# The first residual of a four-layer graph network in one VectorE operation from PSUM, and a new order of work on four engines

## The chip, the cores and the metric

One core of a Trainium2 chip runs the whole program. The metric is the device time of one execution in microseconds (us), median of several. Five parts of the core matter here: TensorE (PE, matrix products; PEld is its weight load), VectorE (DVE), ScalarE (ACT), GpSimd (POOL) and the DMA queue that SyncE (SP) issues. Each runs its own list of instructions strictly in order; a semaphore wait stops everything behind it on that engine.

## The reference, cut to what matters

There are 32 graphs of 256 nodes with 256 features. Each passes four layers, and each layer ends in a residual and a normalization over the features (LN):

```
L0(x)  = (adj @ (x @ W0 + b0)) / rowsum(adj)
L1(x)  = relu((adj @ x) @ W1) * mask(x)
L2(x)  = relu(D^-1/2 (adj + I) D^-1/2 @ x @ W2 + b2),   D = rowsum(adj + I)
L3(x)  = relu(sum over k of  T^k x Wk + bk),  T = rownorm(adj * exp(leaky_relu(attention)))
x = LN(x + L0(x));  x = LN(x + L1(x));  x = LN(x + L2(x));  x = LN(x + L3(x))
```

The change is in the first line of the last group: x + L0(x), before LN. Because every row of adj divided by its row sum adds up to one, b0 can be added to x itself: the kernel computes y0 = (x + b0) + (adj @ (x W0)) / rowsum(adj).

## The kernel before, in words

**Tiles.** A graph is one tile of 128 partitions by 512 columns: two nodes per partition, 256 features each. Eight groups of four graphs ("slots" g = 0 to 3) are worked on. Each fp32 operand of a product is split into a high part (`_hi`, rounded to the fast fp32 format, copied by ScalarE) and a low part (`_lo`, the difference, made by VectorE or GpSimd), and `product` (lines 253 to 263) does lo*hi + hi*lo + hi*hi: 12 matmuls for one 256x256 product.

**Products.** `s1` = x W0, `s2` = adj (x W0) with a column of ones that gives the row sums, `s3`, `s4` = layer 1, `s5`, `s6` = layer 2, `s7` = transposes of x3, `s8a`, `s8b` = x3 by the four weight blocks of layer 3, `s9` = transposes for the attention logits, `s10`, `s11` = the two hops. PSUM has four `ring` banks, one for each slot, and two `pair` tiles of two banks; `pair` is shared in turn by s1, s2, s8a, s8b and s10.

**Stages.** One pass of the loop, `iteration(k)`, does the layers 2 and 3 of group k, the layers 0 and 1 of group k + 1 up to its `s5`, and `s1` of group k + 2. Before it stands `first_iteration` (layers 0 and 1 of group 0), behind it `last_iteration` (layers 2 and 3 of group 7). What sets the order on each engine is a list of calls written out by hand in these functions, one list for each engine; there is no planner in the kernel.

**The first residual.** `sums0` (VectorE, lines 984 to 987) takes the row sums from PSUM and makes the reciprocal `rinv`. `z0` (ScalarE, line 496) multiplies each of the two nodes by its reciprocal on the way from `pair` to X1. `x_bias` (GpSimd, line 751) has added b0 to x in X0, and for group 0 `first_x_bias` (VectorE, line 1065) does. `y0` (GpSimd, line 760) adds X1 to X0. `statistics(0, ...)` (line 975), `variance_eps` (980, 981), `power` (GpSimd, 767) and `norm0` (GpSimd, 782) normalize it to X1, from which `x1_hi` (ScalarE) and `x1_lo` (VectorE, 1008) feed `s3`. `z0_ready` also tells TensorE that a `pair` bank is free: `s2(2)` and `s2(3)` wait for z0 of slots 0 and 1, `s8a(0)` and `s8b(0)` for z0 of slots 2 and 3.

**Names in the rows.** Layers, groups and slots share names: `nod_lo` at line 1013 is `xd_lo` (feeds `s5`), `fea_lo` at 967 is `from_ring` on VectorE, `P<-pair,rinv,P` at 1047 is `q`, `X<-ring,X` at 1060 is `y3`, `adj_lo` at 755 is `adj_lo_part`, `adj_lo` at 806 is `diag_lo`, `mask` at 999 is `mask_of_x1`, `tmp` at 1034 is `leaky`, `W_lo` at 1083 is `weights_lo`, `X<-X,nmr,rstd` at 566 is `norm`.

**SP's queue** in a pass: four loads of xT for group k + 2 (each waits for `s1` of its slot), four of x (each waits for `x1_sum`), four of adj for layer 3, four of adj for group k + 2, and four stores of the output.

Of the kernel before, what the change touches and what calls it, by code (L numbers as in the profile page):

```python
# [25 lines left out]
P = 128  # L26
# [8 lines left out]
def build(nc, x, xT, adjT, w0, w1, w2, wk, wvT, aw, bv, ab, b0, b2, bk, out):  # L35
# [7 lines left out]
    with ExitStack() as ctx:  # L43
# [90 lines left out]
        xT_hi_ready, xT_ready = sem("xT_hi_ready"), sem("xT_ready")  # L134
# [118 lines left out]
        def _(pe):  # L253
# [23 lines left out]
            def s1(g, kn, first=False):  # L277
                pe.wait_ge(xT_ready, count(g, kn))
                if not first:
                    pe.wait_ge(Q_ready, count(2 + g // 2, kn - 2))  # L280
                elif kn == 1:
                    pe.wait_ge(z0_ready, count(2 + g // 2, 0))
# [94 lines left out]
            def first_iteration():  # L377
                for g in (0, 1):
                    s2(g, 0)
                attention_vectors()  # L380
                for g in (2, 3):
                    s2(g, 0)
                for g in (0, 1):
                    s1(g, 1, first=True)
                for g in (0, 1):
                    s3(g, 0, first=True)
                for g in (0, 1):
                    s4(g, 0)
                for g in (2, 3):
                    s3(g, 0, first=True)  # L390
                for g in (2, 3):
                    s4(g, 0)
                for g in (2, 3):
                    s1(g, 1, first=True)
                for g in range(SLOTS):
                    s5(g, 0, first=True)

            def iteration(k, ahead=True):
                for g in (0, 1, 2):
                    s6(g, k)  # L400
# [47 lines left out]
            def last_iteration(k):  # L448
                for g in range(SLOTS):
                    s6(g, k)  # L450
                s7(0, k)
                s8a(0, k, last=True)
                s7(1, k)
                s8b(0, k, last=True)
                s9(0, k)
                s8a(1, k, last=True)
                s7(2, k)
                s8b(1, k, last=True)
                s8a(2, k, last=True)
                s7(3, k)  # L460
                s9(1, k)
# [907 lines left out]
```

## Time and profile before

| | us |
|---|---|
| median of 3 runs (599.04 to 599.85) | 599.43 |
| the profiled execution | 597.33 |
| its span, first to last instruction | 595.5 |
| first `s6(0)` of a group starts, us from the start of the span | 61.09 |
| last one | 541.82 |
| busy: PE, DVE, POOL, ACT | 543.3, 536.2, 471.0, 425.3 |

The span is cut best where TensorE starts `s6(0)`, since that is the start of a pass: 61.09, 130.18, 199.24, 268.35, 337.77, 406.86, 476.84 and 541.82. The first piece is the start with group 0, then come six passes with `s1` ahead, one without, and the last group. Busy time of an instruction is from its start to its end; neighbours on VectorE and ScalarE overlap by about 0.08 us, so a group's busy time is a little more than the time that it takes from the engine. A matmul row of 0.28 us starts 0.12 us after the one ahead of it.

### The profile page before, as it was taken

Reading aid. Unit: us, or ns where it says so; the run is one execution under the profiler, and the core shown is the slowest. Engines: PE = TensorE matmul, PEld = TensorE weight load, DVE = VectorE, ACT = ScalarE, POOL = GpSimd, SP = SyncE. Lnnn points to the kernel's source line nnn. Section 1 sums busy time; section 2 is a strip of 40 time slices with the busy share of each in tenths; the row PEclk is TensorE's granted clock in tenths of the full one; section 3 lists DMA queues with packets and bytes.
Section 4 is the critical chain, followed back from the end, with each engine's and each line's share of the span. In section 5 each row is a group of like instructions: output and inputs, shape, how many; then the busy total and the mean of one; then the engine's idle time right before and its main releaser. Section 6 shows DMA issues by size and latency. Waiting matters only on the chain.

```text
span 595.5 us, 12249 instructions
## 1 busy us (share of the span) xinstructions
PE 543.3 (91%) x4044; PEld 512.1 (86%) x4044; DVE 536.2 (90%) x1213; ACT 425.3 (71%) x937; POOL 471.0 (79%) x575
## 2 busy tenths in 40 slices
PE   5687999999999999999999999998999999987983
PEld 5577998999899998999889998898889998887873
DVE  3779899999999999998999999998999989999666
ACT  5467788488866878578884878667785778756653
POOL 3799699888997799878997889887998788773243
PEclk9979999999999999999999999999999999999998
DMA  8613101431132300322014311324003210101001
GB/s 285 236 56 113 47 19 22 157 101 58 35 106 70 141 18 18 113 98 106 18 36 141 122 35 35 106 70 141 18 18 111 100 37 1 54 19 71 1 1 70
DMA packets 25222, 44.73 MB, mean 75 GB/s; under 512 B 3184, under 2 KB 3824, under 8 KB 25200
## 3 DMA queue, kind: packets, MB, share of 16 engines
q1 hardware_dynamic: 24336, 43.79, 22.1%
q10 hardware_dynamic: 864, 0.66, 0.3%
q8 instruction: 12, 0.20, 0.1%
q14 instruction: 10, 0.08, 0.0%
HBM read 36.05 MB, written 8.39 MB: 75 GB/s over the span
## 4 chain that ended last, share of the span: by engine, by line
PE 36%; DVE 29%; POOL 14%; issue 8%; ACT 8%; DMA 2%; SPq 2%; ACTq 0%; POOLq 0%; DVEq 0%
PE pair L260 8%; PE pair L262 8%; PE pair L261 8%; DVE nod_lo L1013 6%; POOL rstd L767 4%; PE ring L260 4%; ACT X L566 3%; DVE P L1047 3%; PE ring L262 3%; PE ring L261 3%; POOL tmp L789 3%; DVE ring L1055 3%; DVE stats L975 3%; DVE powin L980 2%; DMA xT_in<-xT_dram 2%
## 5 line engine op out<-in xcount | busy, mean ns | idle before, releaser
L767 POOL TENSOR_TENSOR rstd<-powin,minus_half 128x2 f32<-128x2 f32 (+1 forms) x128 | 107.9, 843 | 58.9 <-DVE nmean L981 58.9
L566 ACT ACTIVATE X<-X,nmr,rstd 128x256 f32<-128x256 f32 x192 | 103.5, 592 | 30.4 <-POOL nmr L776 30.1
L975 DVE BATCH_NORM_STATS2 stats<-X 128x6 f32<-128x512 f32 x128 | 89.5, 704 | 1.6 <-POOL X L760 1.2
L260 PE MATMUL ring<-adj_hi,nod_lo 128*128 128x256 f32 x256 | 74.9, 292 | 13.3 <-DVE X L1060 8.1
L260 PE MATMUL ring<-W_hi,fea_lo 128*128 128x256 f32 x256 | 72.5, 283 | 0.9 <-DVE fea_lo L967 0.8
L261 PE MATMUL ring<-adj_lo,nod_hi 128*128 128x256 f32 x256 | 73.0, 285 | 0.0
L262 PE MATMUL ring<-adj_hi,nod_hi 128*128 128x256 f32 x256 | 72.8, 284 | 0.0
L262 PE MATMUL ring<-W_hi,fea_hi 128*128 128x256 f32 x256 | 71.7, 280 | 0.0
L261 PE MATMUL ring<-W_lo,fea_hi 128*128 128x256 f32 x256 | 71.4, 279 | 0.0
L487 ACT ACTIVATE fea_hi<-ring 128x512 fp32r<-128x512 f32 x96 | 55.3, 591 | 22.2 <-PE ring L322 12.2
L967 DVE TENSOR_TENSOR fea_lo<-ring,fea_hi 128x512 fp32r<-128x512 f32 x96 | 63.8, 681 | 2.9 <-ACT fea_hi L487 2.6
L260 PEld LDWEIGHTS ring<-adj_hi,nod_lo 128*128 128x128 f32 x256 | 49.4, 193 | 16.1 <-DVE nod_lo L1013 12.5
L487 ACT ACTIVATE h_hi<-P 128x512 fp32r<-128x512 f32 x32 | 20.2, 633 | 55.1 <-DVE P L1047 55.1
L789 POOL TENSOR_TENSOR tmp<-tmp,adj_in 128x512 f32<-128x512 f32 x32 | 47.3, 1486 | 14.6 <-ACT tmp L551 14.6
L1013 DVE SCALAR_TENSOR_TENSOR nod_lo<-X,rstd,nod_hi 128x256 fp32r<-128x256 f32 x64 | 53.8, 882 | 1.3 <-ACT nod_hi L528 1.0
L260 PE MATMUL pair<-WB_hi,fea_lo 128*128 128x512 f32 x128 | 53.5, 418 | 0.2 <-DVE h_lo L995 0.2
L755 POOL TENSOR_TENSOR adj_lo<-adj_in,adj_hi 128x512 fp32r<-128x512 f32 x32 | 40.8, 1298 | 14.6 <-ACT adj_hi L487 14.6
L261 PE MATMUL pair<-WB_lo,fea_hi 128*128 128x512 f32 x128 | 50.6, 395 | 0.0
L760 POOL TENSOR_TENSOR X<-X 128x512 f32<-128x512 f32 x32 | 45.2, 1412 | 6.6 <-ACT X L496 5.9
L262 PE MATMUL pair<-WB_hi,fea_hi 128*128 128x512 f32 x128 | 50.4, 394 | 0.0
L260 PEld LDWEIGHTS ring<-W_hi,fea_lo 128*128 128x128 f32 x256 | 48.2, 188 | 1.7 <-issue 1.3
L261 PEld LDWEIGHTS ring<-adj_lo,nod_hi 128*128 128x128 f32 x256 | 49.6, 194 | 0.0
(109 smaller groups left out, 2125.8 us busy)
## 6 DMA issues: line engine op xcount, KB each, us to landing
adj_in<-adjT_dram SPq DMA_DIRECT2D x64, 256.0 KB, 3.2
xT_in<-xT_dram SPq DMA_DIRECT2D x32, 256.0 KB, 3.5
X<-x_dram SPq DMA_DIRECT2D x32, 256.0 KB, 2.6
out_dram<-X SPq DMA_DIRECT2D x32, 256.0 KB, 2.0
P<-wk_dram SPq DMA_DIRECT2D x3, 256.0 KB, 8.4
P<-w_dram SPq DMA_DIRECT2D x2, 256.0 KB, 8.0
X<-bk_dram SPq DMA_DIRECT2D x3, 128.0 KB, 7.8
P<-w_dram ACTq DMA_DIRECT2D x1, 256.0 KB, 3.9
```

The source lines that it names most:

```text
L260: mm(o, lhs(1, t, i), rhs(0, t), start=t == 0, stop=False)
L261: mm(o, lhs(0, t, i), rhs(1, t), start=False, stop=False)
L262: last = mm(o, lhs(0, t, i), rhs(0, t), start=False, stop=t == 1)
L487: return nc.scalar.activation(dst, src, ACT.Copy)
L566: last = nc.scalar.activation(nodes(X[min(l + 1, 3)][g])[:, t, :], nodes(X[l][g])[:, t, :], ACT.Identity, scale=rstd[l][g][:, t:t + 1], bi ...
L755: tt(adj_lo[g][:, :], adj_in[g][:, :], adj_hi[g][:, :], ALU.subtract).then_inc(adj_ready, 1)
L760: tt(X0[g][:, :], X0[g][:, :], X1[g][:, :], ALU.add).then_inc(y_ready[0][g], 1)
L767: tt(rstd[l][g][:, 0:n], powin[l][g][:, 0:n], minus_half[:, 0:n], ALU.pow).then_inc(rstd_ready[l], 1)
L789: tt(tmp[g][:, :], tmp[g][:, :], adj3_in[g][:, :], ALU.mult).then_inc(al_ready, 1)
L967: tt(fea_lo[g][:, :], ring[g][:, :], fea_hi[g][:, :], ALU.subtract).then_inc(ready, 1)
L975: nc.vector.bn_stats(stats[l][g][:, :], by_turns(X[l][g])).then_inc(st_ready[l], 1)
L1013: last = stt(nod_lo[g][:, t * F:(t + 1) * F], nodes(X2[g])[:, t, :], rstd[0][g][:, 2 + t:3 + t], nod_hi[g][:, t * F:(t + 1) * F], ALU.mult ...
```

## The change: what it does

`z0` on ScalarE and `y0` on GpSimd go. VectorE has a new `y0` of two operations: pair * rinv + X0, written over X0. It waits for `rinv0_ready` (made by its own `sums0`) and for the bias addition; `y0_done` takes the place of `z0_ready` and of `y_ready[0]` everywhere. The bias additions of group 0 count in a semaphore of their own, as do the first four low parts of xT. All calls of the four engines stand in a new order.

```diff
 # VectorE
+            def y0(g, kn, first=False):
+                dve.wait_ge(rinv0_ready, count(g, kn))
+                if first:
+                    dve.wait_ge(first_xb_ready, g + 1)
+                else:
+                    dve.wait_ge(xb_ready, count(g, kn - 1))
+                for t in range(2):
+                    half = nodes(X0[g])[:, t, :]
+                    last = stt(half, pair[g % 2][:, t, 0:F], rinv[g][:, t:t + 1], half, ALU.mult, ALU.add)
+                last.then_inc(y0_done, 1)
 # ScalarE
-            def z0(g, kn):
-                act.wait_ge(rinv0_ready, count(g, kn))
-                for t in range(2):
-                    last = nc.scalar.activation(nodes(X1[g])[:, t, :], pair[g % 2][:, t, 0:F], ACT.Identity,
-                                                scale=rinv[g][:, t:t + 1])
-                last.then_inc(z0_ready, 1)
 # GpSimd
-            def y0(g, kn):
-                pool.wait_ge(xb_ready, count(g, kn))
-                pool.wait_ge(z0_ready, count(g, kn))
-                tt(X0[g][:, :], X0[g][:, :], X1[g][:, :], ALU.add).then_inc(y_ready[0][g], 1)
 # TensorE: s2(2), s2(3); s8a(0), s8b(0) and the first s1 ahead in the same way
                 if g >= 2:
-                    pe.wait_ge(z0_ready, count(g - 2, kn))
+                    pe.wait_ge(y0_done, count(g - 2, kn))
```

The new order, as the calls now follow each other (n = k + 1; a number or letter in brackets is the slot, `..` a row of slots; "ring" is `from_ring`, "var" `variance_eps`, "stat" `statistics`, "ms" `mean_scale`):

```
TensorE, a pass: s6(0) s6(1) s2(0,n) s6(2) s2(1,n) s2(2,n) s7(0) s6(3) s2(3,n) s7(1) s8a(0) s8b(0) s9(0)
  s8a(1) s7(2) s3(0,n) s8b(1) s8a(2) s4(0,n) s9(1) s9(2) s7(3) s8b(2) s8a(3) s3(1,n) s9(3) s3(2,n) s8b(3)
  s4(1,n) s4(2,n) s10(0) s10(1) s3(3,n) s10(2) s4(3,n) s10(3) s11(0) s11(1) s11(2) s1(0) s1(1) s11(3)
  s5(0,n) s5(1,n) s1(2) s5(2,n) s5(3,n) s1(3)
VectorE, start of a pass: h_lo(0..2) y2(0) y2b(0) h_lo(3) stat(2,0) y2(1) sums0(0) y2b(1) var(2,0) y0(0)
  y2(2) stat(2,1) stat(0,0) sums0(1) sums0(2) var(2,1) var(0,0) y0(1) y0(2) ring(x3T,0) y2b(2) sums0(3)
  y0(3) stat(2,2) var(2,2) stat(0,1) p0(0) ...
VectorE, end of a pass: ... q(3) var(1,3) z3(0) y3(0) z3(1) stat(3,0) z3(2) y3(1) y3(2) stat(3,1) xd_lo(0)
  var(3,0) var(3,1) xd_lo(1) stat(3,2) z3(3) var(3,2) xd_lo(2) y3(3) stat(3,3) var(3,3) xd_lo(3) ring(t2,0..3)
ScalarE, start: h_hi(0) h_hi(1) h_hi(2) adj_hi(0) xT_hi(0) h_hi(3) adj_hi(1..3) norm(2,0) ring(x3T,0) norm(2,1)
  x1_hi(0) x1_sum(0) ...
ScalarE, end: ... norm(3,0) ring(t2,0) ring(t2,1) norm(3,1) norm(3,2) norm(3,3) ring(t2,2) ring(t2,3)
GpSimd, end: ... diag_lo(1) diag_lo(2) q_lo(3) diag_lo(3) xT_lo(3) power(3,0) power(3,1) ms ms power(3,2)
  x_bias(0) ms power(3,3) ms x_bias(1..3)          (before: x_bias(0) in mid-pass, x_bias(1) and xT_lo(3)
  between the powers of slots 1 and 2, x_bias(2), x_bias(3) last)
first_iteration, TensorE: attention_vectors s2(0) s2(1) s2(2) s1(0) s3(0) s2(3) s3(1) s4(0) s4(1) s3(2) s3(3)
  s4(2) s4(3) s1(1) s1(2) s5(0..3) s1(3)      (before: s2(0..1) attention_vectors s2(2..3) s1(0..1) s3(0..1)
  s4(0..1) s3(2..3) s4(2..3) s1(2..3) s5(0..3))
first_iteration, VectorE: h_lo(0..3) attention_constants sums0(0) x_bias(0) y0(0) stat(0,0) sums0(1) var(0,0)
  x_bias(1) x_bias(2) sums0(2) y0(1) y0(2) stat(0,1) stat(0,2) x1_lo(0) var var x_bias(3) weights_lo
  mask(0) sums0(3) x1_lo(1) ring(t1,0) y0(3) ...
first_iteration, GpSimd: adj_lo(0) adj_lo(1) diag_sum(0) diag_sum(1) adj_lo(2) adj_lo(3) diag_sum(2)
  diag_sum(3) power(0,0) norm0(0) xT_lo(0) power(0,1) norm0(1) ...
first_iteration, ScalarE: ... xT_hi(0) xT_hi(1) x1_hi(0) weights_hi x1_hi(1) ...
```

`last_iteration` is reordered in small ways (`s7(1)` ahead of `s8a(0)`, `s9(1)` ahead of `s8a(2)`, `exp(0)` ahead of the copies behind it, `y2(3)` ahead of the first copy from the ring).

## Rows read from the trace of the kernel before

**Rows 1.** Windows by stage: stretch, length, busy by engine, granted clock, DMA, GB/s.
```profile
0.00:61.09 61.09, 43.14 (x300) 40.59 (x301) 42.48 (x92) 35.52 (x80) 43.42 (x55) 0.92 0.51 173
...
268.35:337.77 69.42, 66.56 (x507) 63.13 (x505) 65.96 (x149) 52.35 (x117) 60.21 (x73) 1.00 0.23 76
...
541.82:595.50 53.68, 38.68 (x265) 34.77 (x264) 38.16 (x87) 27.46 (x53) 17.52 (x26) 0.96 0.08 30
```

**Rows 2.** Timeline of TensorE: the first matmuls of s6(0) and, twelve later, s6(1).
```profile
268.35 0.28 PE L260 MATMUL ring<-W_hi,fea_lo 128*128 128x256 f32 x1
...
269.76 0.28 PE L260 MATMUL ring<-W_hi,fea_lo 128*128 128x256 f32 x1
```

**Rows 3.** Longest wait of TensorE in the pass 268.35 to 337.77: total, times, longest.
```profile
PE ring L260 <- DVE X L1060: 1.3, 1, 1.3
```

**Rows 4.** Waits of VectorE in the same pass.
```profile
DVE ring L1021 <- PE ring L262: 1.1, 1, 1.1
DVE P L1030 <- PE pair L262: 0.9, 2, 0.5
```

**Rows 5.** Groups by form in that pass, VectorE: count, busy us, mean ns.
```profile
L975 DVE BATCH_NORM_STATS2 stats<-X 128x6 f32<-128x512 f32 x16 | 11.2, 705 | 0.0
...
L1013 DVE SCALAR_TENSOR_TENSOR nod_lo<-X,rstd,nod_hi 128x256 fp32r<-128x256 f32 x8 | 7.1, 932 | 0.0
L980 DVE TENSOR_SCALAR powin<-stats 128x2 f32<-128x2 f32 x16 | 5.8, 360 | 0.1
L991 DVE TENSOR_TENSOR alpha_lo<-tmp,alpha_hi 128x512 fp32r<-128x512 f32 x4 | 3.8, 963 | 0.0
...
L999 DVE TENSOR_SCALAR mask<-absum 128x2 f32<-128x2 f32 x4 | 1.7, 436 | 0.0
```

**Rows 6.** By tile, whole trace: shortest, median, longest ns.
```profile
L1013 DVE SCALAR_TENSOR_TENSOR nod_lo<-X,rstd,nod_hi x64: 464/484/1581, 51.6 to 539.0; 128x256 fp32r<-128x256 f32 x64
L980 DVE TENSOR_SCALAR powin<-stats x128: 145/159/1275, 21.9 to 590.3; 128x2 f32<-128x2 f32 x128
L991 DVE TENSOR_TENSOR alpha_lo<-tmp,alpha_hi x32: 677/680/1280, 94.2 to 577.5; 128x512 fp32r<-128x512 f32 x32
L1047 DVE SCALAR_TENSOR_TENSOR P<-pair,rinv,P x64: 465/476/485, 104.3 to 582.5; 128x256 f32<-128x256 f32 x64
```

**Rows 7.** Groups by form in the pass of rows 5, GpSimd.
```profile
L760 POOL TENSOR_TENSOR X<-X 128x512 f32<-128x512 f32 x4 | 5.6, 1408 | 0.9 <-ACT X L496 0.9
L782 POOL TENSOR_SCALAR X<-X,nmean,rstd 128x256 f32<-128x256 f32 x8 | 5.6, 710 | 0.7 <-POOL rstd L767 0.7
...
L767 POOL TENSOR_TENSOR rstd<-powin,minus_half 128x4 f32<-128x4 f32 x4 | 4.1, 1013 | 0.5 <-DVE nmean L981 0.5
```

**Rows 8.** Timeline, VectorE and GpSimd: start, duration, near 262 and near 290.
```profile
261.82 2.86 DVE L1013 SCALAR_TENSOR_TENSOR nod_lo<-X,rstd,nod_hi 128x256 fp32r<-128x256 f32 x2
262.92 1.47 POOL L793 TENSOR_TENSOR xT_lo<-xT_in,xT_hi 128x512 fp32r<-128x512 f32 x1
289.98 1.20 DVE L980 TENSOR_SCALAR powin<-stats 128x2 f32<-128x2 f32 x1
289.87 1.29 POOL L760 TENSOR_TENSOR X<-X 128x512 f32<-128x512 f32 x1
```

**Rows 9.** Timeline of the start: ScalarE, VectorE, TensorE.
```profile
20.71 0.63 ACT L487 ACTIVATE xT_hi<-xT_in 128x512 fp32r<-128x512 f32 x1 [3.83 <-DMA xT_in<-xT_dram]
18.07 0.69 DVE L1065 TENSOR_TENSOR X<-X,b_bc 128x512 f32<-128x512 f32 x1 [2.08 <-DMA X<-x_dram]
24.93 0.42 DVE L1078 TENSOR_TENSOR bk_bc<-X,X 128x256 f32<-128x256 f32 x1
30.91 0.15 DVE L1083 TENSOR_TENSOR WA_lo<-P,WA_hi 128x4 fp32r<-128x4 f32 x1
33.83 0.58 PE L260 MATMUL ring<-adj_hi,nod_lo 128*128 128x256 f32 x1 [1.61 <-DVE nod_lo L1008]
37.18 0.58 PE L260 MATMUL ring<-adj_hi,nod_lo 128*128 128x256 f32 x1 [0.41 <-DVE nod_lo L1008]
```

More of the change, by code:

```diff
@@ L277, in s1 @@
             def s1(g, kn, first=False):
-                pe.wait_ge(xT_ready, count(g, kn))
+                if first and kn == 0:
+                    pe.wait_ge(first_xT_ready, g + 1)
+                else:
+                    pe.wait_ge(xT_ready, count(g, kn - 1))
                 if not first:
@@ L651, in iteration @@
                 x1_hi(1, k + 1)
+                x1_sum(1, k + 1)
+                x1_hi(2, k + 1)
+                x1_hi(3, k + 1)
+                p12(2, k)
+                exp(1, k)
+                logits(3, k)
+                exp(2, k)
+                alpha_hi_part(0, k)
+                from_ring(1, s3_done, k + 1, fea_hi, t1_hi_ready)
+                from_ring(2, s3_done, k + 1, fea_hi, t1_hi_ready)
+                exp(3, k)
+                alpha_hi_part(1, k)
+                if ahead:
+                    xT_hi_part(2, k + 2)
@@ L652, in iteration @@
+                p12(3, k)
+                alpha_hi_part(2, k)
+                x1_sum(2, k + 1)
+                x1_sum(3, k + 1)
+                diag_hi(1, k + 1)
+                alpha_hi_part(3, k)
+                q_hi(0, k)
+                from_ring(3, s3_done, k + 1, fea_hi, t1_hi_ready)
                 if ahead:
                     xT_hi_part(3, k + 2)
-                for g in (0, 1):
-                    exp(g, k)
-                logits(2, k)
-                x1_hi(2, k + 1)
-                x1_sum(1, k + 1)
@@ L721, in last_iteration @@
                 alpha_hi_part(3, k)
-                for g in (1, 2, 3):
-                    q_hi(g, k)
-                for g in range(SLOTS):
-                    norm(3, g, k)
+                q_hi(1, k)
+                q_hi(2, k)
+                q_hi(3, k)
+                norm(3, 0, k)
+                norm(3, 1, k)
+                norm(3, 2, k)
+                norm(3, 3, k)
             act.dma_start(W0_in, w0.rearrange("p (t f) -> p t f", t=2)).then_inc(w0_loaded, 16)
@@ L922, in iteration @@
                 if ahead:
-                    for g in (2, 3):
-                        x_bias(g, k + 2)
+                    x_bias(1, k + 2)
+                    x_bias(2, k + 2)
+                    x_bias(3, k + 2)
             def last_iteration(k):
@@ L934, in last_iteration @@
                 mean_scale(2, 3, k)
-                for g in range(SLOTS):
-                    alpha(g, k)
-                for g in range(SLOTS):
-                    q_lo(g, k)
-                for g in (0, 1):
-                    power(3, g, k)
-                for g in (0, 1):
-                    mean_scale(3, g, k)
+                alpha(0, k)
+                alpha(1, k)
+                alpha(2, k)
+                alpha(3, k)
+                q_lo(0, k)
+                q_lo(1, k)
+                q_lo(2, k)
+                q_lo(3, k)
+                power(3, 0, k)
+                mean_scale(3, 0, k)
+                power(3, 1, k)
+                mean_scale(3, 1, k)
                 power(3, 2, k)
@@ L1239, in iteration @@
+                variance_eps(3, 2, k)
                 xd_lo(2, k + 1)
-                statistics(3, 2, k)
-                xd_lo(3, k + 1)
                 y3(3, k)
-                variance_eps(3, 2, k)
                 statistics(3, 3, k)
                 variance_eps(3, 3, k)
-                for g in range(SLOTS):
-                    from_ring(g, t2_hi_ready, k + 1, t2_ready)
+                xd_lo(3, k + 1)
+                from_ring(0, t2_hi_ready, k + 1, t2_ready)
+                from_ring(1, t2_hi_ready, k + 1, t2_ready)
```

591 lines of the change are left out of this document (300 added, 291 removed).

## The prediction

> **What bounds the kernel now.** Read the windows by stage first [rows 1]: in a pass of 69.42 us TensorE is busy 66.56 us, VectorE 65.96, GpSimd 60.21, ScalarE 52.35. Two engines are full within 5%, so neither share alone says which one is the limit. The six full passes take 69.1 to 70.0 us; with the start (61.09 us) and the last group (53.68 us) they make the span. In these two pieces TensorE works only 43.14 and 38.68 us: they are chains of waits, and the start can be shortened by order alone.
>
> Next, the waits within a pass. TensorE's 69.42 - 66.56 = 2.9 us of idle time has one large part, 1.3 us, where `s5(3)` waits for `y3(3)` on VectorE [rows 3]. VectorE's 69.42 - 65.96 = 3.5 us are mostly waits for TensorE: 1.1 us at the start of the pass (`y2(0)`), 0.9 us in two pieces for P0 [rows 4]. So the end of a pass is bound by VectorE, its first third by TensorE.
>
> Third, durations. Four groups of VectorE are longer than they need be [rows 5, 6]: nod_lo takes 932 ns where the median of the trace is 484, powin 360 against 159, alpha_lo 963 against 680, mask 436 against some 160. The timeline tells why: the powin at 289.98 takes 1.20 us and ends at 291.18, when GpSimd's addition (289.87 + 1.29 = 291.16) ends; the second of the pair of nod_lo from 261.82 ends at 264.68, behind a GpSimd subtraction that ends at 264.39 [rows 8]. The forms with one PSUM operand do not do this: the 64 `q` operations range from 465 to 485 ns [rows 6]. In one pass the holding costs 8 x 0.45 + 16 x 0.20 + 4 x 0.28 + 4 x 0.28 = 9.0 us, with about 0.6 us in smaller groups 9.6 us. VectorE's own work is thus 65.96 - 9.6 = 56.4 us of a pass; the rest depends on what GpSimd does beside it.
>
> **The change in a full pass.** *VectorE's new operations.* Eight a pass, 128x256, out of PSUM, with a scalar and an SBUF operand that is also the output: exactly the form of `q`, 476 ns [rows 6], of which 0.08 us overlap with the next. That is 8 x 0.40 = 3.2 us. Bounds: 8 x 0.48 = 3.8 us without any overlap; below 3.0 us there is no row of such a form. They lie on an engine that is full, so they count in whole where VectorE is the limit.
>
> The Trainium skill, "VectorE: DVE Perf Modes", section on the TRN2 errata, gives (120 + 256)/0.96 = 392 ns for such an operation; an estimate by that page would be 8 x 0.39 = 3.1 us. The row of this case is 476 ns for start to end, and the sum goes by the rows.
>
> *What goes.* ScalarE's eight scaled copies: ScalarE has 17 us free in a pass, so their time is worth nothing; what counts is that the residual no longer waits in ScalarE's list. GpSimd's four additions, 5.6 us [rows 7]: GpSimd is not full either. But they held VectorE: the powin above lost 1.04 us to one. If holding goes with GpSimd's busy time, 9.6 x 5.6/60.2 = 0.9 us are saved. The other end is one full addition for each of the four, 4 x 1.3 = 5.2 us.
>
> The Trainium skill, "SBUF — State Buffer", section Who interferes with whom, says that the port pair of VectorE and GpSimd is an exclusive lock, taken for a whole instruction, and that a VectorE instruction with at most one SBUF input stays out of it. By that rule the new form never waits, as the rows of `q` show, and each removed GpSimd operation can free VectorE for its whole length, which is the 5.2 us end; the other reading of the same rule is that GpSimd's next instruction simply moves into the place of the removed one and nothing is saved.
>
> *The new order and the holding.* I followed both lists through a pass. At its end, x_bias(1..3) now stand behind the last power, beside the four ring copies and the next h_lo, which read PSUM and are not held; before, the last two loads of this kind (x_bias(1), xT_lo(3)) ran beside xd_lo(3) and cost it 2 us [rows 8]. Against that, x_bias(0) moves to the end (1.3 us, beside xd_lo(2) or y3(3)), and leaky(1), x1_lo(2) and alpha_lo(1) meet powers, norms and alpha on GpSimd. Summed where the lists meet, I come to about 7.5 us of holding; by share of busy time it is 9.6 - 0.9 = 8.7. I take 8.
>
> *Sum for a pass.* VectorE: 56.4 + 3.2 + 8.0 = 67.6 us, plus its idle time. Of the 3.5 us idle, the 1.1 us at the start is filled (three h_lo's now stand in front of y2(0)) and the waits for sums0 by the y0's; the waits for P0 and for the logits stay. I take 1.4 us: 69.0 us against 69.3 as the mean of the six. Ends: TensorE's own 66.6 us plus some 0.5 us that single switches cost, 67.1; and with all 3.5 us of idle, and 9.6 of holding, 72.7.
>
> *Added waits.* `s2(2)` waits for `y0(0)`, eleven VectorE operations into the pass. By the durations above y0(0) ends 7.0 to 7.3 us after `s6(0)` starts; TensorE comes to `s2(2)` after five products of 1.41 us [rows 2], at 7.1. Behind the wait stand s7(0), s6(3) and s2(3), and behind s7(0) the whole of layer 3. Likewise `s2(3)` (y0(1) at about 10.4, its turn at 10.4), `s8a(0)` (y0(2), 1 us early), `s8b(0)` (y0(3), 0.4 us early). At most 0.3 us is lost in a pass while VectorE keeps up; it is in the 0.5 us. On ScalarE, xT_hi(0) now stands ahead of h_hi(3), on which `s2(1)` hangs. SP issues that load behind the store of slot 3; norm(3,3) now comes ahead of two ring copies, so store and load go some 2 us earlier against `s6(0)`; a wait of 0.8 us there is covered, since s2(1)'s turn comes after four products, 5.6 us, and h_lo(3) is ready at 3.9.
>
> There are seven passes between the first and the last `s6(0)`: 7 x -0.3 = -2 us; ends 7 x -2.2 = -15 and 7 x +3.4 = +24, of which I use +1.5 a pass, +10, as the practical end, since holding and idle time fill each other.
>
> **The change at the start.** Before, ScalarE stood 3.83 us before xT_hi(0) until its load came [rows 9], with z0(1) behind it, and z0(2) behind the weight copies; `s3(0)` began at 33.83, `s3(1)` at 37.18. Now the residual of slot 0 needs only the bias addition, which begins at 18.07 when x has come [rows 9]: y0(0) ends at 18.07 + 0.6 + 0.8 = 19.5, statistics 0.7 and variance 0.2 [rows 5, 6], power 1.0 and norm0 1.4 [rows 7]: x1(0) is there at about 22.8, some 9 us earlier. But `weights_lo` (24.93 to 31.06, 6.1 us [rows 9]) stays in VectorE's list ahead of x1_lo(1), the first ring copies and y0(3). It begins at about 26, so x1_lo(1) ends near 32 to 32.5 and `s3(1)` starts 5 us earlier than before. From there on the chain has the same links; two products of `s1` (1.4 us each) move behind `s4(3)`, into idle time of TensorE (18 us in this piece). At the end of the piece x_bias(1), x_bias(2) and diag_lo can still hold xd_lo, as before. I take 5.5 us gained, bounds 1 (the weights eat it) and 9 (x1(0) itself). attention_vectors first costs nothing: its loads land before the last `s1(3)` ends, by the order in which ScalarE's queue issues them.
>
> **The last group.** Small moves in a chain with 15 us of idle on TensorE: y2(3) before the ring copy delays s8a(0) by up to 0.8 us, exp(0) earlier saves about 1. I take -0.5, bounds -3 and +2.
>
> **Sum.** -2 - 5.5 - 0.5 = -8 us on the profiled execution: 597.3 - 8 = 589.3 (span 587.5). The median before is 2.1 us above that execution, so the forecast for the median is 599.4 - 8 = 591.4.
>
> **Rivals.**
> - *A, VectorE becomes the limit (slower).* The 3.2 us come in whole and the holding does not fall (9.6 us stay, or GpSimd's lighter list only moves its instructions against others). VectorE then has 69.2 us of work in a pass, and with 1.6 us of waits a pass is 70.8, +1.5: 7 x 1.5 = +10.5, less 5.5 at the start: 604. It decides from 0.8 us more a pass on. For it: the engine has only 3.5 us free and the y0's stand in TensorE's way. Against it: the places of x_bias, and the four additions that did hold it. Chance 0.20.
> - *B, TensorE's floor.* The order removes nearly all of the 2.9 us: a pass of 67.3, 7 x -2.0 = -14, and -6: 579. For it: without holding, my walk through the lists leaves TensorE almost no wait. Against: 8 us of holding have to find places where VectorE waits anyway, and it waits only 3.5. Chance 0.17. An end as low as 5.2 us of holding saved lands here too.
> - *C, the start gives nothing.* weights_lo or the tail of xd_lo takes the gain, passes as forecast: 599.4 - 2 - 0.5 = 597. Chance 0.13. The same time would come if the start gains and the passes lose 0.5 us.
> - The forecast: 0.50, own range 585 to 597.
>
> **How the numbers follow.** A measurement of this kernel can tell 0.2%, 1.2 us. Faster by more: the forecast (0.50), B (0.17), and a bit over half of C (0.08): 0.75. Within 0.2%: 0.06, from C and the edge of A. Slower: A and its tails, 0.19. The range takes in B down to 580 and most of A up to 603.
>
> **What would show it.** After the change: a y0 row of VectorE, 64 operations near 476 ns with no long ones; the first `s3` near 25 to 27 instead of 33.8 and the first `s6(0)` near 55.5 instead of 61.1; passes near 69.0; nod_lo's mean below 932 ns, powin's near 330; VectorE busy about 67.6 us in a pass and GpSimd 54.6. Wrong would be: passes over 70 with TensorE waiting for y0 or ring copies (A), passes at 67.3 (B), a first `s6(0)` at 60 (C), or TensorE in `s2(2)` waiting more than 0.5 us a pass.

## The result, and the profile after

| | us |
|---|---|
| changed kernel, median of 4 runs (573.40 to 578.12) | 575.61 |
| kernel before, 4 runs beside them (598.31 to 599.85) | 599.23 |
| ratio, 95% interval | 0.961 [0.956, 0.966] |
| the profiled execution of the changed kernel; its span | 576.90; 575.1 |

The kernel is 24 us faster, where 8 were forecast; the time lies below the forecast range. `s6(0)` starts at 60.10, 125.88, 192.08, 258.31, 324.60, 390.76, 457.00 and 521.36 us. By pieces, against the starts given before:

| piece | before | after | forecast |
|---|---|---|---|
| start | 61.09 | 60.10 | -5.5 |
| mean of the six passes with `s1` ahead | 69.29 | 66.15 | -0.3 each |
| the pass without | 64.98 | 64.36 | |
| last group | 53.68 | 53.74 | -0.5 |

So the six passes bring 18.9 of the 20.4 us of span. The windows by stage of the changed kernel (stretch, length, busy by engine, granted clock, DMA, GB/s), to set beside [rows 1]:

```profile
0.00:60.10 60.10, 44.49 (x300) 42.84 (x301) 40.00 (x101) 33.22 (x75) 38.66 (x51) 0.89 0.51 169
...
258.31:324.60 66.29, 65.91 (x506) 63.19 (x505) 61.84 (x157) 48.38 (x109) 52.94 (x69) 1.00 0.24 79
521.36:575.10 53.74, 38.78 (x266) 34.57 (x264) 37.67 (x86) 26.03 (x50) 17.73 (x24) 0.95 0.07 27
```

VectorE has eight operations more in a pass (157 against 149) and is busy 4.1 us less. The groups by form in that pass (count, busy us, mean ns) say where, beside [rows 5]:

```profile
L1031 DVE SCALAR_TENSOR_TENSOR nod_lo<-X,rstd,nod_hi 128x256 fp32r<-128x256 f32 x8 | 3.6, 492 | 0.0
...
L1004 DVE SCALAR_TENSOR_TENSOR X<-pair,rinv,X 128x256 f32<-128x256 f32 x8 | 3.4, 470 | 0.1
...
L987 DVE TENSOR_SCALAR powin<-stats 128x2 f32<-128x2 f32 x16 | 2.7, 173 | 0.4
...
L1009 DVE TENSOR_TENSOR alpha_lo<-tmp,alpha_hi 128x512 fp32r<-128x512 f32 x4 | 2.7, 686 | 0.0
...
L1017 DVE TENSOR_SCALAR mask<-absum 128x2 f32<-128x2 f32 x4 | 0.6, 162 | 0.0
```

The four groups that were held in [rows 5] are at their own length: 932 to 492 ns, 360 to 173, 963 to 686, 436 to 162. Summed over all groups of a pass, count times (mean less the shortest mean that the same group has in any of the kernels below), VectorE's holding is 9.9 us before (9.6 by the prediction's own count) and 1.4 after. This sum is called "holding" below. The new operation by tile, whole trace (shortest, median, longest ns), is the form that the prediction took it for [rows 6]:

```profile
L1004 DVE SCALAR_TENSOR_TENSOR X<-pair,rinv,X x64: 462/474/486, 19.8 to 470.2; 128x256 f32<-128x256 f32 x64
```

The waits in the pass (total us, times, longest), beside [rows 3, 4]; first TensorE's only one of a size:

```profile
PE pair L260 <- DVE X L1004: 0.3, 1, 0.3
```

then VectorE's three largest:

```profile
DVE tmp L1052 <- ACT tmp L550: 1.4, 2, 1.2
DVE fea_lo L971 <- ACT fea_hi L499: 1.1, 2, 0.9
DVE X L1022 <- PE ring L262: 0.5, 1, 0.5
```

TensorE's row is full (65.91 of 66.29). It looks like rival B, TensorE's floor. The experiments say that it isn't (e8, e9).

### The profile page after: what moved, and what is told of

Read it like the earlier page. It is cut to its first block, busy times and chain, and to the rows that moved or that the text cites. A ratio compares the mean times of both kernels' runs of the same rounds, so it can differ in the third digit from the quotient of the medians.

```text
span 575.1 us, 12181 instructions
## 1 busy us (share of the span) xinstructions
PE 539.7 (94%) x4044; PEld 514.4 (89%) x4044; DVE 508.2 (88%) x1277; ACT 394.1 (69%) x873; POOL 416.7 (72%) x543
## 4 chain that ended last, share of the span: by engine, by line
PE 62%; DVE 22%; issue 5%; ACT 3%; DMA 3%; POOL 2%; SPq 2%; DVEq 0%; ACTq 0%; POOLq 0%
PE pair L260 13%; PE pair L262 12%; PE pair L261 12%; PE ring L260 8%; PE ring L262 7%; PE ring L261 7%; DVE stats L982 5%; DVE ring L1073 4%; DVE X L1078 2%; DVE nod_lo L1031 2%; PE ring L325 2%; POOL rstd L772 1%; ACT X L571 1%; DMA xT_in<-xT_dram 1%; DMA X<-x_dram 1%
## 5 line engine op out<-in xcount | busy, mean ns | idle before, releaser
L499 ACT ACTIVATE fea_hi<-ring 128x512 fp32r<-128x512 f32 x96 | 53.4, 588 | 14.0 <-PE ring L325 7.2
L794 POOL TENSOR_TENSOR tmp<-tmp,adj_in 128x512 f32<-128x512 f32 x32 | 44.5, 1399 | 20.5 <-ACT tmp L556 20.5
L802 POOL TENSOR_TENSOR h_lo<-P,h_hi 128x512 fp32r<-128x512 f32 x32 | 38.7, 1211 | 22.4 <-ACT h_hi L499 22.4
L260 PE MATMUL pair<-WB_hi,fea_lo 128*128 128x512 f32 x128 | 51.5, 403 | 0.0
L262 PEld LDWEIGHTS ring<-adj_hi,nod_hi 128*128 128x128 f32 x256 | 49.9, 195 | 0.0
```

The source lines that it names most:

```text
L260: mm(o, lhs(1, t, i), rhs(0, t), start=t == 0, stop=False)
L262: last = mm(o, lhs(0, t, i), rhs(0, t), start=False, stop=t == 1)
L499: return nc.scalar.activation(dst, src, ACT.Copy)
L794: tt(tmp[g][:, :], tmp[g][:, :], adj3_in[g][:, :], ALU.mult).then_inc(al_ready, 1)
L802: tt(mixed(h_lo[g])[:, :, 0:F], nodes(P1[g]), mixed(h_hi[g])[:, :, 0:F], ALU.subtract).then_inc(Q_lo_ready, 1)
```

## The experiments

"Pass" is the length between two `s6(0)` in mid-run, "holding" the sum above for that pass.

| kernel | median us | ratio to before [95%] | pass | VectorE busy | holding |
|---|---|---|---|---|---|
| before | | 1 | 69.4 | 65.96 | 9.9 |
| changed | 575.6 | 0.961 [0.956, 0.966] | 66.3 | 61.84 | 1.4 |
| e1, operation alone | 607.8 | 1.015 [1.012, 1.019] | 70.4 | 66.63 | 7.3 |
| e2, order alone | 609.9 | 1.019 [1.016, 1.022] | 70.6 | 59.88 | 2.3 |
| p3_pool, GpSimd's old list | 645.0 | 1.082 [1.075, 1.089] | 77.0 | 68.42 | 7.4 |
| p5_pe, TensorE's old list | 622.2 | 1.041 [1.038, 1.045] | 72.6 | 61.25 | 0.6 |
| g1_xbias | 593.0 | 0.993 [0.990, 0.996] | 69.3 | 64.89 | 4.6 |
| e7_extra_pool | 602.4 | 1.007 [1.004, 1.009] | 69.9 | 66.08 | 5.3 |
| e8_pad4 | 595.6 | 0.996 [0.994, 0.998] | 68.8 | 65.00 | 1.8 |
| e8_pad8 | 611.4 | 1.023 [1.021, 1.026] | 71.0 | 67.44 | 2.0 |
| e9_less_pe | 575.4 | 0.963 [0.961, 0.964] | 66.1 | 61.69 | 1.2 |
| f1_less_dve | 574.5 | 0.961 [0.957, 0.964] | 66.2 | 61.00 | 2.4 |
| f2_less_both | 574.0 | 0.959 [0.955, 0.963] | 66.1 | 60.93 | 2.3 |
| h2_tail_both | 572.4 | 0.957 [0.953, 0.960] | 65.9 | 61.15 | 1.7 |
| h4_s2_both | 569.7 | 0.951 [0.948, 0.954] | 65.6 | 60.50 | 2.1 |

### Operation or order: e1 and e2

e1 has the new functions and, on all four engines, the calls in their old order; in VectorE's list only this is added (and the same behind each of the other `sums0`):

```diff
 sums0(0, k + 1)
+y0(0, k + 1)
```

> The new operation alone: VectorE makes the first residual from PSUM, ScalarE's copies and GpSimd's additions are gone, and every engine works through the order of the kernel before (y0 stands right behind the sums of its slot). T (the order of the lists gives the gain, the operation by itself is neutral): passes stay at 69 to 70 us, VectorE's nod_lo stays over 800 ns and powin over 300 ns, median 597 to 603. R1 (the operation gives it: four GpSimd instructions fewer to hold VectorE, and a shorter way to the residual): passes of 67 us or less, nod_lo under 650 ns, median under 586.

e2 is the reverse: all lists new, `z0` back on ScalarE (`z0(0)` behind `adj_hi(2)`, `z0(1)` behind `adj_hi(3)`, `z0(2)` and `z0(3)` behind `norm(2,0)` and `norm(2,1)`) and `y0` on GpSimd (`y0(0)` and `y0(1)` behind the mean scales of layer 2, `y0(2)` behind `diag_sum(0)`, `y0(3)` behind `power(0,1)`).

> The new order alone: all four lists as in the changed kernel, but the residual is made as before, by ScalarE's scaled copy and GpSimd's addition, which stand in those lists at the places nearest to their old ones. T: passes of 66.3 to 67.2 us, since VectorE is held little in the new order (nod_lo under 650 ns, powin under 220 ns), median 576 to 583. R1: the four additions hold VectorE again or come late for the statistics, passes of 68.5 us or more, median over 592.

Measured: each half alone makes the kernel slower, by 1.5% and 1.9%; together they make it 3.9% faster. For e1 theory T is near but too kind: pass, nod_lo, powin and median each lie just outside its numbers, and far from R1's. The row by stage and the two groups:

```profile
272.99:343.42 70.43, 67.11 (x506) 63.25 (x505) 66.63 (x157) 49.14 (x109) 54.48 (x69) 1.00 0.23 74
...
L1028 DVE SCALAR_TENSOR_TENSOR nod_lo<-X,rstd,nod_hi 128x256 fp32r<-128x256 f32 x8 | 6.1, 799 | 0.0
L984 DVE TENSOR_SCALAR powin<-stats 128x2 f32<-128x2 f32 x16 | 4.7, 294 | 0.1
```

This is rival A of the prediction, found in another kernel: y0 comes in whole, VectorE's 66.63 us and 3.8 idle are the pass, 70.4 us (A was priced at 70.8). It also prices the removed GpSimd additions: with the order unchanged, holding falls from 9.9 to 7.3, so 2.6 us for four of them, 0.65 each. For e2, T's mechanism shows (nod_lo 493 ns, powin 228, holding 2.3), but pass and median are R1's. Little holding alone thus doesn't make a pass short. The likely reason is R1's second half, that a residual which goes through two more engines comes late for an order made for one; VectorE's longest wait for GpSimd in this pass, 0.9 us ahead of a statistics operation, is only a part of it. TensorE's wait in its pass:

```profile
PE ring L326 <- ACT X L579: 3.0, 1, 3.0
```

The 3.0 us are `s7` waiting for a norm of ScalarE, in whose list I had put the z0's. With other places for them e2 could do better, which wasn't tried; so e2 shows what this placing costs, and not the least that the order alone can do.

### Whose list: p3_pool, p5_pe, g1_xbias

p3_pool and p5_pe are the changed kernel with one engine's lists for the passes and the last group as before. g1_xbias moves three calls of GpSimd:

```diff
+x_bias(0, k + 2)
 alpha(3, k)
...
-xT_lo_part(3, k + 2)
 power(3, 0, k)
...
-power(3, 2, k)
-x_bias(0, k + 2)
+x_bias(1, k + 2)
+xT_lo_part(3, k + 2)
+power(3, 2, k)
```

> The changed kernel with GpSimd's list in the passes (and in the last group) in the order of before; the other three lists and the start are new. T, in the form that the holding depends on which GpSimd instruction stands beside which of VectorE: the holding comes back in part, nod_lo over 700 ns, a pass of 67.5 to 69.5, median 585 to 598. Rival (the holding fell because VectorE's own list changed, x_bias to the end, and GpSimd's list matters little): nod_lo about 500 ns, a pass under 66.8, median 575 to 580.

> The changed kernel with TensorE's list in the passes (and in the last group) in the order of before; the other three lists and the start are new. T: the products come in another order than VectorE takes them, single switches cost TensorE 0.2 to 1.5 us a pass, a pass of 66.5 to 67.7, median 577 to 586, and nod_lo stays under 650 ns. R2 (TensorE's list is what brings the gain): a pass of 68.5 or more, median over 591.

> The changed kernel with three GpSimd instructions of a pass put back where they stood before: x_bias(0) ahead of the last alpha, x_bias(1) and xT_lo(3) ahead of power(3,2), where they ran beside xd_lo(3). T (which GpSimd instruction stands beside which of VectorE decides the holding, and VectorE's order is what a pass waits for): VectorE's busy time rises from 61.8 by 2 to 3 us in a pass, a pass of 68 to 69.5 us, median 588 to 598. Rival (these three are harmless, the holding went with the rest of GpSimd's list): a pass under 67 us, median under 581.

Measured: GpSimd's old list brings 6.0 us of holding back, more on powin (390 ns) than on nod_lo (607, where T said over 700), and costs far more than T said, 10.7 us a pass, since it also comes late (TensorE waits 2.4 us for GpSimd's h_lo, and 2.5 us for `q` on VectorE). TensorE's old list leaves VectorE unheld (0.6) and still costs 6.3 us a pass. T's range, up to 67.7, is missed by far. It is R2's number, but not its proof: a pass of 72.6 is longer than before, so what is seen is a list that doesn't fit the other three. VectorE's and ScalarE's lists weren't put back alone. g1 is as T said: three calls cost 3.0 us a pass and 17.4 us in all. Its timeline at the end of a pass, VectorE and then GpSimd:

```profile
324.80 1.11 DVE L987 TENSOR_SCALAR powin<-stats 128x2 f32<-128x2 f32 x1
...
325.90 1.92 DVE L1031 SCALAR_TENSOR_TENSOR nod_lo<-X,rstd,nod_hi 128x256 fp32r<-128x256 f32 x2
```

```profile
324.60 1.29 POOL L761 TENSOR_TENSOR X<-X,b_bc 128x512 f32<-128x512 f32 x1
325.85 1.30 POOL L798 TENSOR_TENSOR xT_lo<-xT_in,xT_hi 128x512 fp32r<-128x512 f32 x1
```

The powin ends when x_bias(1) ends (325.89), the first nod_lo 0.3 us after the end of xT_lo(3) (327.15): 2 us at the one place where the pass ends on VectorE. The changed kernel has its three bias additions there beside ring copies instead.

### The holding by itself: m1_lock

> No part of the model is computed, only the disputed cost is measured: 14 stretches, each with ten operations of one form on VectorE, or six on GpSimd, or both beside each other. Forms of VectorE: 128x256 with two SBUF operands (nod_lo of layer 2), 128x512 with two SBUF operands (nod_lo of layer 1), 128x256 with a PSUM and an SBUF operand (y0 and q), 128x512 with a PSUM and an SBUF operand (the ring copies), 128x2 (powin). Of GpSimd: the 128x512 addition, the 128x256 normalisation. T (the two hold each other up for whole instructions, whichever came later waits): with two SBUF operands the two engines' stretches add up, VectorE's operations vary between their own length and that plus 1.3 us, and GpSimd's grow too; with a PSUM operand both run as if alone (0.48 and 0.69 us against 1.29). Rival (they share and slow each other evenly): all rows grow by a like factor in every stretch, those with a PSUM operand too.

The timeline, VectorE, first each form alone, then six additions of GpSimd beside it (start, duration of ten operations):

```profile
7.17 4.05 DVE L91 SCALAR_TENSOR_TENSOR nod<-d_in,sc 128x256 fp32r<-128x256 f32 x10 [6.27 <-ACT ring L79]
...
17.88 4.01 DVE L97 SCALAR_TENSOR_TENSOR x0n<-ring,sc,d_in 128x256 f32<-128x256 f32 x10 [0.28 <-POOL psc L139]
22.17 0.79 DVE L103 TENSOR_SCALAR powin<-mixed_in 128x2 f32<-128x2 f32 x10 [0.28 <-POOL psc L139]
...
34.59 10.11 DVE L91 SCALAR_TENSOR_TENSOR nod<-d_in,sc 128x256 fp32r<-128x256 f32 x10
...
57.44 4.01 DVE L97 SCALAR_TENSOR_TENSOR x0n<-ring,sc,d_in 128x256 f32<-128x256 f32 x10
...
72.33 5.12 DVE L103 TENSOR_SCALAR powin<-mixed_in 128x2 f32<-128x2 f32 x10 [1.45 <-POOL padd L127]
...
79.83 4.63 DVE L91 SCALAR_TENSOR_TENSOR nod<-d_in,sc 128x256 fp32r<-128x256 f32 x10 [2.38 <-POOL padd L127]
```

and GpSimd's six normalisations alone and beside the last of these:

```profile
31.04 3.23 POOL L130 TENSOR_SCALAR padd<-p_in,psc 128x256 f32<-128x256 f32 x6 [0.33 <-DVE sc L112]
...
79.97 5.29 POOL L130 TENSOR_SCALAR padd<-p_in,psc 128x256 f32<-128x256 f32 x6 [0.18 <-POOL padd L127]
```

T is confirmed beside additions: with two SBUF operands 4.05 us become 10.11; with one in PSUM 4.01 stay 4.01. The tiny powin, with a single SBUF operand, goes from 0.79 to 5.12. By tile an operation is either free (470 ns) or about 1.0 us longer (1476 in the median), most of the 1.26 us of one addition, and not slowed a little:

```profile
L91 DVE SCALAR_TENSOR_TENSOR nod<-d_in,sc x10: 470/1476/1522, 34.6 to 44.2; 128x256 fp32r<-128x256 f32 x10
...
L103 DVE TENSOR_SCALAR powin<-mixed_in x10: 154/166/1248, 72.3 to 77.3; 128x2 f32<-128x2 f32 x10
```

The Trainium skill, "SBUF — State Buffer", section Who interferes with whom, says that whoever issues first has the shared pair for the whole instruction and that `tensor_scalar` within SBUF can enter a mode that needs it; the trace agrees that a held operation waits in one piece (1476 ns against 470) and that a `tensor_scalar` is held (powin's 1248); in which mode it ran no row shows. My sentence in the prediction, that an operation with at most one SBUF input stays out, left this exception away. It holds in the other direction as well: GpSimd's normalisation goes from 3.23 to 5.29 us for six. Beside these normalisations VectorE loses little, 4.63 us for 4.05, so who pays depends on the pair.

### What holds a pass at 66.2: e7, e8, e9, f1, f2, h2, h4

e7 computes `xT_lo` twice. e8 repeats statistics. e9 and f2 leave a term of `s1` out, f1, f2, h2 and h4 shorten statistics, h4 leaves a term of `s2` out. The edits in the helpers:

```diff
 # e7, GpSimd's xT_lo_part
+tt(xT_lo[g][:, :], xT_in[g][:, :], xT_hi[g][:, :], ALU.subtract).then_inc(extra_done, 1)
+pool.wait_ge(extra_done, count(g, kn - 1))
 # e8, VectorE's statistics (pad4: l == 2, pad8: l in (1, 2))
+if l == 2:
+    nc.vector.bn_stats(spare[:, :], by_turns(X[l][g]))
 # e9, f2, h2 (both=False in s1), h4 (in s2), TensorE's product
-mm(o, lhs(0, t, i), rhs(1, t), start=False, stop=False)
+if both:
+    mm(o, lhs(0, t, i), rhs(1, t), start=False, stop=False)
 # f1, f2, h4 (l in (1, 2)), h2 (l == 3)
-nc.vector.bn_stats(stats[l][g][:, :], by_turns(X[l][g]))
+nc.vector.bn_stats(stats[l][g][:, :], by_turns(X[l][g])[:, 0:128])
```

> The changed kernel with GpSimd work put back in the amount of the four additions that went: each `xT_lo_part` is computed twice (four more 128x512 operations of 1.29 us a pass, 5.2 us). F (a pass is TensorE's own 65.9 us and GpSimd's amount of work is not what counts): a pass of 66.2 to 66.8 us, median 575 to 580. Rival H (each added operation holds VectorE for its length or pushes the GpSimd instructions behind it against others of VectorE): VectorE goes from 61.8 to 64 to 67 us busy in a pass, a pass of 67.5 us or more, median over 584.

> The changed kernel with four needless statistics operations more a pass on VectorE (0.70 us each at most, 0.62 where they follow one another: 2.5 to 2.8 us; their result is not used). F: VectorE has 66.3 - 61.8 = 4.4 us free in a pass, so a pass stays at 66.2 to 66.8 us, median 575 to 580. Rival V (TensorE's waits are short only because VectorE is just in time, its order leaves no slack): the pass grows by 1.5 to 2.8 us, median 586 to 595.

> The same with eight a pass, 5.0 to 5.6 us: more than the 4.4 us that VectorE has free. F: VectorE is now just the limit, a pass of 67.0 to 68.5 us, median 581 to 592. V: the pass grows by nearly all of it, 70.5 us or more, median 605 or more.

> The changed kernel with less work for TensorE: the feature product `s1` leaves out its term of high part times low part, 16 of its 48 matmuls in a pass of four slots (its results are a little less exact), 1.9 us a pass. F: a pass is shorter by 1.3 to 1.9 us, 64.4 to 65.0, median 561 to 567 with some of it in the start. V: VectorE's order sets the pass, it shortens by less than 0.5 us, median 571 or more.

I expected F, TensorE's floor, and all four runs speak against it. Rows by stage of e8_pad4 and e9:

```profile
263.38:332.20 68.82, 66.75 (x506) 63.23 (x505) 65.00 (x161) 48.37 (x109) 53.55 (x69) 1.00 0.23 76
```

```profile
254.38:320.52 66.14, 64.65 (x491) 61.45 (x489) 61.69 (x157) 48.36 (x110) 52.92 (x69) 1.00 0.25 79
```

With four statistics more VectorE is busy 3.2 us more and the pass is 2.5 us longer (e8_pad8: 5.6 and 4.7), although VectorE is idle 4.5 us in a pass of the changed kernel; 1.3 us less on TensorE make it no shorter. e7's four GpSimd operations add 3.9 us of holding and 3.6 to the pass. So VectorE's idle time, which is mostly a wait for ScalarE in the midst of its chain, is hardly slack: of the 4.5 us only 0.6 and 0.9 took up the added work. But VectorE alone isn't the limit either:

> The changed kernel with less work for VectorE: the statistics of layers 1 and 2 are taken from half of the columns (the results are less exact for it), 8 operations a pass that are some 0.27 us shorter, 2.1 us. TensorE's work is whole. D (both engines are tight in a pass, each at its own places): TensorE has no wait left to lose, the pass stays at 65.9 to 66.3 us, median 572 to 576. V (VectorE's order alone sets the pass, TensorE's row only looks full because its instructions spread): a pass of 64.0 to 65.0 us, median 559 to 567.

> The same, and TensorE's `s1` without its term of high part times low part (1.4 to 1.9 us a pass less). D: only now is the pass shorter, 64.2 to 65.0 us, median 560 to 568. V: the same time as with less work for VectorE alone, within 2 us.

Neither shortens the pass (66.2 and 66.1). Part is a matter of size: of the 2.2 us taken off the statistics holding takes 1.0 back, VectorE is busy only 0.84 us less. The rest of VectorE's list then meets other instructions of GpSimd. In f2 TensorE waits at three places, which are the candidates for what is late next:

```profile
PE ring L260 <- DVE nod_lo L1033: 0.8, 2, 0.4
PE pair L260 <- POOL adj_lo L766: 0.4, 1, 0.4
PE pair L260 <- DVE X L1006: 0.2, 1, 0.2
```

`s5` waits for xd_lo, as `s1` ahead of it is shorter but VectorE's tail is not; `s2(0)` for GpSimd's adj_lo, which stands behind the bias additions; `s2(2)` for y0. The last two kernels relieve both engines in one stretch.

> The changed kernel with both engines relieved in the same stretch, the last quarter of a pass: the statistics of layer 3 are taken from half of the columns (4 operations of 0.44 instead of 0.70 us a pass, 1.0 us, less exact results), and TensorE's `s1` has no term of high part times low part (1.4 us, as in e9). S (each stretch of a pass has its own limit: TensorE and VectorE in the first 52 us, VectorE's tail, TensorE kept up by `s1`, behind it; what was relieved in e9 and f2 was relieved where the other engine was the limit): a pass of 65.0 to 65.5 us, median 565 to 569. Rival R (some other cycle, a load or GpSimd's list, holds the pass at 66.1): a pass of 66.0 to 66.2, median 573 to 576.

> The changed kernel with both relieved in the first 52 us of a pass: the statistics of layers 1 and 2 from half of the columns, as in f1, and TensorE's `s2` without its term of high part times low part (16 matmuls a pass, 1.4 to 1.9 us; both make the results less exact). S: now the first stretch is shorter and with it the pass, 64.4 to 65.3 us, median 561 to 568. R: 66.0 to 66.2 us, median 573 to 576.

Passes of 65.9 and 65.6: 0.4 and 0.6 us less, between the two theories' numbers. That fits limits by stretch (S) if behind each the next one stands within some 0.6 us, but no run shows these next limits. Which cycle holds h4 at 65.6, with TensorE idle 1.3 and VectorE 5.1 us, is left open; TensorE's largest wait there is 0.9 us for y0. Nor was it tested whether a load or GpSimd's list holds the pass at 66.1 to 66.2.

### The start: a2_again, s1_split, s2_split_x, s3_x

s1_split and s2_split_x, s3_x are new orders of the start; a2_again is the changed kernel once more.

```diff
 # s1_split, s2_split_x: VectorE, first_iteration
-weights_lo()                                    # six subtractions
+weights_lo()                                    # W1 alone
...
 from_ring(1, t1_hi_ready, 0, t1_ready)
+weights_part(3, 6)                              # WB, WA's last columns
...
 from_ring(3, t1_hi_ready, 0, t1_ready)
+weights_part(1, 3)                              # W2, WA
 # s2_split_x, s3_x: SP
+for g in range(SLOTS):
+    load_x(g, 0, before=False)
 for tile, dram in c_loads:
```

> The changed kernel with another order of one thing at the start, exact results: of `weights_lo` (4.1 us on VectorE at 28.2 to 32.3) only the part of W1 stays there, the five other subtractions stand behind the ring copies of slots 1 and 3. H (VectorE's two-operand subtractions hold GpSimd: norm0(1) takes 3.04 us beside them where norm0(0) takes 1.09): norm0(1) falls to 1.1 to 1.7 us, the second `s3` starts 1.5 to 3 us earlier than in the kernel it is made from (33.8 to 35.2), first `s6(0)` at 54.5 to 56.5, median 572 to 575. Rival (the chain at the start hangs on the loads, not on VectorE's list): first `s6(0)` stays at 56.7 to 60.1, median 574.5 to 577.

> The same, and the four loads of x stand ahead of those of the weights in SP's list, exact results. H: the first bias addition starts at 16 to 17 us instead of 18.6, first `s3` at 25 to 26.5, first `s6(0)` at 53 to 55.5, median 570 to 574. Rival (the load of x is not what comes last: the next adjacency, xT or the weights are, and they now come later): no earlier than s1_split, within 1 us of it or later.

> The changed kernel once more, nothing edited, for a second profiled execution. C (the 5.5 us of the start were there, and the granted clock took most of them back in the one profiled execution: 0.52 from 34 to 38 us and 0.63 from 38 to 42, where the kernels with the same start and a clock of 1.00 there reach the first `s6(0)` at 56.6 to 57.5): with a clock of 1.00 at 34 to 42 us the first `s6(0)` is at 56.5 to 57.5, with a clock near half there at 60 to 62; the second `s3` at 33.5 to 35.5. Rival (the kernels that reached 56.7 owe it to their own edits): first `s6(0)` at 60 whatever the clock. Passes of 66.2 us and a median of 573.5 to 577 for both.

> The changed kernel with one thing moved, exact results: the four loads of x stand ahead of those of the weights in SP's list; `weights_lo` is whole and at its place. H: the first bias addition starts 0.5 to 1.5 us earlier than at 18.1 to 18.6, the chain behind it too, median 0.5 to 1.5 us under that of the unedited changed kernel. Rival (the first `s2` is what the chain waits for, the load is not last): no difference, within 0.5 us.

| kernel | median us | ratio [95%] | second `s3` | first `s6(0)` | clock 34 to 38, 38 to 42 |
|---|---|---|---|---|---|
| changed | 575.6 | 0.961 [0.956, 0.966] | 35.22 | 60.10 | 0.52, 0.63 |
| a2_again | 575.5 | 0.958 [0.956, 0.960] | 33.96 | 57.79 | 0.63, 1.00 |
| s3_x | 575.1 | 0.958 [0.956, 0.959] | 33.35 | 56.26 | 1.00, 1.00 |
| s1_split | 579.0 | 0.966 [0.963, 0.969] | 33.27 | 61.81 | 0.68, 1.00 |
| s2_split_x | 578.5 | 0.964 [0.961, 0.967] | 32.91 | 59.97 | 1.00, 1.00 |

C, the theory of a2_again's expectation, holds in the main: the same kernel starts its passes 2.3 us earlier in the second profiled execution, at a clock between C's two cases. Of these 2.3 us 1.3 are there when the second `s3` starts, behind a stretch (22 to 26 us) with a clock of 0.76 in the first and 1.00 in the second execution. The rows by stage from 34 to 42 us, of the first one and then of s3_x (the column behind GpSimd's busy time is the granted clock):

```profile
34.00:38.00 4.00, 2.78 (x13) 2.78 (x14) 3.59 (x10) 1.15 (x4) 3.91 (x4) 0.52 0.23 66
38.00:42.00 4.00, 4.00 (x24) 4.00 (x24) 1.91 (x4) 3.54 (x10) 2.10 (x3) 0.63 0.00 0
```

```profile
34.00:38.00 4.00, 3.55 (x30) 3.38 (x29) 3.83 (x8) 1.94 (x4) 3.65 (x5) 1.00 0.02 6
38.00:42.00 4.00, 3.29 (x28) 3.09 (x27) 3.56 (x10) 3.25 (x13) 3.81 (x6) 1.00 0.24 55
```

TensorE does 37 matmuls in these 8 us at 1.2 GHz for most of the time, 58 at 2.4. It had been idle for 3.2 us ahead of the second `s3`, which starts at 35.22 and takes 2.73 us instead of 1.54; `s4(0)` behind it takes 2.56. Three other kernels with this very start, p5_pe, g1_xbias and e8_pad4, had a clock of 1.00 from 34 us on and their first `s6(0)` at 56.63 to 56.75; p3_pool, a fourth, had 0.66 from 34 to 38 us and got there at 57.55. The wait alone doesn't decide the clock: it is 2.4 us in a2_again and p3_pool, where the clock is low behind it, and just as long in g1_xbias and e8_pad4, where it is 1.00. What decides it is open. Against the 61.09 of before, the start is worth 4.4 us where the clock stays up, 3.3 in a2_again, and 1.0 in the first profiled execution. But the kernel before ran at 0.50 and 0.53 from 30 to 38 us in its only profiled execution, so part of the 4.4 us may be clock as well. a2_again gives 1.5 us back in the last group, where the clock is 0.87 in a stretch of 10 us that has 1.00 in the first execution; so the time saved at the start doesn't show in the spans (575.1 and 574.6).

s1_split: H is right about the holding and wrong about the time. GpSimd's norm0(1), and the two `xT_lo` behind norm0(2):

```profile
28.11 1.09 POOL L788 TENSOR_SCALAR X<-X,nmean,rstd 128x256 f32<-128x256 f32 x2 [0.18 <-POOL rstd L773]
...
31.40 2.96 POOL L799 TENSOR_TENSOR xT_lo<-xT_in,xT_hi 128x512 fp32r<-128x512 f32 x2
```

1.09 us instead of the 3.04 of the changed kernel. But GpSimd's xT_lo then stands beside x1_lo(1), which takes 1.78 us instead of 0.69, and the subtractions that were moved make `s5(0)` wait 2.5 us for xd_lo. The kernel is 0.6% slower than the changed one. The load of x ahead of the weights moves the first bias addition from 18.1-18.6 to 17.6 and the median by 0.4 us, which the runs can't tell from nothing. No version here beats the changed kernel.

## Why the prediction was wrong

- *VectorE's new operations*: right. 64 of 474 ns, 3.4 us a pass (3.2 foreseen).
- *The new order and the holding*: this is the step that failed, in the forecast's term of 8.0 us of holding. "I take 8" should have been 1.4. The four removed additions were within their bounds (2.6 us, between 0.9 and 5.2), but for the order I let less than 1 us go, and it takes away 5.9 (7.3 in e1, 1.4 in the changed kernel). I looked for pairs that meet and found some on either side; g1 shows what that walk missed: three calls are worth 3.2 us of holding and 3.0 us a pass. The walk had seen the 2 us on xd_lo in the tail and set x_bias(0) at its new place against them; but 2.1 of the 3.2 us are on powin (305 ns for 173), which it didn't price there, and 1.0 on nod_lo. The error was to treat holding as a share of GpSimd's busy time with small corrections. It is a sum over pairs of instructions, and an order can be free of nearly all.
- *Sum for a pass*: the form was right, VectorE's work and holding and idle time; in e7 and g1, 3.9 and 3.2 us more of holding make a pass 3.6 and 3.0 us longer. A small sum of holding is not enough, though: e2 and p5_pe have 2.3 and 0.6 us, and passes of 70.6 and 72.6. By terms: holding -6.6 against the forecast, idle time +3.1 (4.5, not 1.4), own work +0.8: -2.7, and 69.0 becomes 66.3. The bound of 67.1, "TensorE's own 66.6 plus 0.5", was too high: the same products, busy 66.6 us in [rows 1], fill 65.9 here and 67.5 in p5_pe, at a clock of 1.00 in each. TensorE's busy time in a pass is no fixed amount of work.
- *Added waits*: right. `s2(2)` waits 0.3 us for y0(0), no other.
- *The start*: the first `s3` came at 27.4 (25 to 27 foreseen), the second at 35.2 (32), the first `s6(0)` at 60.1 (55.5). Right: y0(0) in place of ScalarE's copy, and that weights_lo stands in the way. Not foreseen: that it does so by holding GpSimd's norm0(1) (3.04 us for 1.1; with that gone, s1_split's second `s3` is at 33.3), and a clock of 0.52 and 0.63 from 34 to 42 us. Rival C's sign, a first `s6(0)` at 60, came out in the first profiled execution, in part by the clock, which C didn't name; in a2_again it was at 57.8.
- *The last group*: 0, -0.5 foreseen.
- *The rivals*: B had the nearest time (579) and the wrong mechanism, since TensorE's floor isn't what holds the pass (e9). That its time is near is luck: it took 6 us from the start, which gave 1.0, and too little from the passes. A is what the operation does without the order (e1). In the passes I gave the better end a chance of 0.17, because I took the 3.5 us of VectorE's idle time as the place where any relief had to fit.

## What to carry to other kernels

Where an engine is over 90% busy, split its busy time into own length and holding before pricing a new order: group by form, take count times (mean less shortest), and look for the partner instruction whose end frees the held one. Price a new order of two such engines by walking pair by pair, and give "nearly all of it goes" a real chance. A list of calls is tuned as a set: one engine's list, or the operation alone, put into the other's surroundings made the kernel 1.5 to 8% slower than before. Idle time on a full engine is slack only if adding work there costs nothing.

## What the runs showed of the hardware that I had not expected

- An operation of 128x2 on VectorE with a single SBUF operand is held nearly as long as a large one: 154 ns at its shortest, up to 1248 beside an addition of GpSimd (128x256 with two SBUF operands: 470 and 1522).
- VectorE holds GpSimd too: norm0 3.04 us for 1.09 beside weights_lo, and six normalisations 5.29 us for 3.23, while VectorE's ten operations beside them take 4.63 for 4.05.
- The same kernel reached its first pass at 60.1 us with a granted clock of 0.52 and 0.63 from 34 to 42 us (1.2 GHz for most of it), and at 57.8 with 0.63 and 1.00. A wait of 2.4 us ahead of it was followed by either clock (0.63 in a2_again, 1.00 in g1_xbias).
